# One-hots of a degree count in pairs of edge tiles, in a graph network kernel

## The chip, the cores and the metric

The kernel runs on one core of one Trainium2 chip. The metric is the device time of one execution in microseconds (us). A core has five engines with queues of their own: TensorE (PE, with its weight loads listed as PEld), VectorE (DVE), ScalarE (ACT), GpSimd (POOL) and SyncE (SP, which issues DMAs). They meet only at semaphores. SBUF, the on-chip memory, has 128 partitions.

## The reference

A graph of 12,500 nodes and 200,000 edges, sorted by destination, goes through two residual blocks: three layers of graph convolution, and one layer with edge features.

```python
loop = jnp.arange(N, dtype=message_edge.dtype)
src = jnp.concatenate([message_edge[0], loop])
dst = jnp.concatenate([message_edge[1], loop])
deg = jax.ops.segment_sum(jnp.ones_like(dst, dtype=jnp.float32), dst, num_segments=N)
dinv = jnp.where(deg > 0, jax.lax.rsqrt(deg), 0.0)
norm = dinv[src] * dinv[dst]
x = jax.nn.relu(_gcn_conv(node_embed, W1, b1, src, dst, norm))
# ... two more layers; then the layer with edge features:
msg = hv[src] * filt
h = jax.ops.segment_sum(msg, dst, num_segments=N_NODES)
return jax.nn.silu(h @ W_post.T + b_post)
```

The part that matters here is `deg`: how many edges end in each node.

## The kernel before, in words

Edges are laid out in tiles of 128, one edge per partition; 8 tiles (`BLOCK_TILES`) make a block, and there are 196 blocks (`BLOCKS`). A node number is split into a window (number / 128, 98 of them, `WINDOWS`) and a remainder (number mod 128).

After the loads and some integer arithmetic on VectorE (L846 to L875), the first long stage counts degrees. For every block VectorE writes two one-hot arrays in bf16 (loop at L878, through the helper `tile_hots`, whose instructions all stand at L695): `rem_hot`, 128 remainders for each of 8 tiles (1,024 elements a partition), and `win_hot`, 98 windows for each of 8 tiles (784 elements). Each compares a constant, `iota_block`, with the numbers of the block's edges (`dst_rem`, `dst_win`, one number per partition and tile). TensorE then multiplies, tile by tile, the remainders' one-hot (the weights, 128x128) with the windows' one-hot (the moving operand, 98 columns) and sums all 1,568 tiles in one PSUM area, `ps_deg` (`deg_block`, L1347 to L1352): the count of edges for each remainder and window.

In both arrays the tile index is the innermost one: element (n, k) of tile k stands at 8n + k. Tile k's operand is thus read at a step of 8 elements, 16 bytes.

The array `hot` has room for two blocks (index `a`). VectorE waits with `deg_used` until TensorE is done with the block two before; TensorE waits with `deg_hot` until VectorE has written the block. The constant `iota_block` (value n at every (n, k)) is written by GpSimd at L488 before anything else; it lies in the memory of `onehot_more`, by which name the profile lists it.

Behind the loop, in VectorE's program, come a short chain (L889 to L923), the copy of the counts, a layer norm and the first projection; then the dense stage with sub-window tables, whose helper is `tile_hots` again, with one or two tiles at a time (`src_extra`, `src_main`, on `stage_fn`, compared with `src_rem` from a first tile that is read from a table). Their order on TensorE, in a loop over 25 pairs of windows, does not depend on the degree count's layout. L1376 multiplies those arrays, L1389 the fp8 counts made from them; L1233 transposes node features before the projections at L1247.

Of the kernel before, what the change touches and what calls it, by code (L numbers as in the profile page):

```python
# [23 lines left out]
BF16 = mybir.dt.bfloat16  # L24
# [3 lines left out]
ALU = mybir.AluOpType  # L28
# [4 lines left out]
P = 128  # L33
NODES, EDGES, D, RADIAL = 12500, 200000, 64, 50
WINDOWS = -(-NODES // P)
# [5 lines left out]
BLOCK_TILES = 8  # L41
# [37 lines left out]
def gnn_program(nc, x, src, dst, radial, W1, b1, W2, b2, W3, b3, W_pre, b_pre, W_rad, b_rad, W_post, b_post, out):  # L79
    ctx = ExitStack()  # L80
    with ctx:
# [3 lines left out]
        def sem(name):  # L85
            return ctx.enter_context(nc.semaphore(name))

        def cut(buffer, at, n):

            return buffer[:, at:at + n]  # L90
# [30 lines left out]
        dst_rem = cut(ring, 2 * TILES, TILES // 2).bitcast(BF16)  # L121
        dst_win = cut(ring, 3 * TILES, TILES // 2).bitcast(BF16)
# [5 lines left out]
        hot = sbuf("hot", [P, 2 * BLOCK_TILES * SPAN])  # L128
        onehot = hot[:, :].rearrange("p (a k n) -> p a k n", a=2, n=SPAN)
        onehot16 = cut(hot, 0, BLOCK_TILES * SPAN).bitcast(BF16).rearrange("p (a k n) -> p a k n", a=2, n=SPAN)  # L130
        rest = cut(hot, BLOCK_TILES * SPAN, BLOCK_TILES * D).rearrange("p (k f) -> p k f", f=D)
        rem_hot = cut(hot, 0, BLOCK_TILES * P).bitcast(BF16).rearrange("p (a n k) -> p a n k", a=2, n=P)
        win_hot = cut(hot, BLOCK_TILES * P, BLOCK_TILES * WINDOWS).bitcast(BF16).rearrange(
            "p (a n k) -> p a n k", a=2, n=WINDOWS)
        stage_nf = cut(hot, 0, 2 * GROUP * D).rearrange("p (h w f) -> p h w f", h=2, f=D)
        gated = stage_nf
        onehot_more = sbuf("onehot_more", [P, BLOCK_TILES, MORE])
        more_flat = onehot_more[:, :, :].rearrange("p k n -> p (k n)")
        iota_block = cut(more_flat, 0, P * BLOCK_TILES // 2).bitcast(BF16).rearrange("p (n k) -> p n k", n=P)
        rel_more = sbuf("rel_more", [P, BLOCK_TILES])  # L140


# [45 lines left out]
        base = sbuf("base", [1, BLOCKS], I32)  # L188
# [33 lines left out]
        ps_deg = ps[:, 0, 0:WINDOWS]  # L222
# [21 lines left out]
        deg_hot = sem("deg_hot")  # L244
# [231 lines left out]
        @block.gpsimd  # L476
        def _(pool):

            nc.gpsimd.memset(xs[:, WINDOWS - 1, :], 0.0).then_inc(xs_cleared, 1)
            nc.gpsimd.memset(ident[:, :], 0.0).then_inc(consts_made, 1)  # L480
            nc.gpsimd.memset(one[:, :], 1.0).then_inc(consts_made, 1)
            nc.gpsimd.memset(found[:, :], 0.0).then_inc(consts_made, 1)
            nc.gpsimd.memset(sub_table[:, 2 * SUBS:], 0).then_inc(consts_made, 1)
            nc.gpsimd.iota(iota_i[:, 0:SPAN], pattern=[[1, SPAN]], base=0, channel_multiplier=0).then_inc(consts_made, 1)
            nc.gpsimd.iota(iota_i[:, SPAN:SPAN + WINDOWS], pattern=[[MORE, WINDOWS]], base=SPAN,
                           channel_multiplier=0).then_inc(consts_made, 1)

            nc.gpsimd.iota(iota_block, pattern=[[1, P], [0, BLOCK_TILES]], base=0, channel_multiplier=0,  # L488
                           allow_small_or_imprecise_dtypes=True).then_inc(consts_made, 1)
            nc.gpsimd.iota(sub_start[:, :], pattern=[[STRIDE, SUBS]], base=0, channel_multiplier=0,  # L490
                           allow_small_or_imprecise_dtypes=True).then_inc(consts_made, 1)
            nc.gpsimd.iota(block_no, pattern=[[1, BLOCKS]], base=0, channel_multiplier=0,
                           allow_small_or_imprecise_dtypes=True).then_inc(consts_made, 1)
            pool.wait_ge(consts_made, N_CONSTS - 1)
            nc.gpsimd.affine_select(out=ident[:, :], in_=ident[:, :], compare_op=ALU.not_equal, fill=1.0,
                                    base=0, pattern=[[-1, P]], channel_multiplier=1).then_inc(consts_made, 1)

            pool.wait_ge(block_range, 2)
            nc.gpsimd.partition_all_reduce(range_p1, range_p, P, REDUCE.max).then_inc(range_all, 1)

            pool.wait_ge(z_used, (PROJECT(0) + 1) * GROUPS + 2)
            nc.gpsimd.iota(iota_joint, pattern=[[1, JOINT]], base=0, channel_multiplier=0,
                           allow_small_or_imprecise_dtypes=True).then_inc(turns_made, 1)
            nc.gpsimd.iota(iota_main, pattern=[[1, P], [0, MAIN]], base=0, channel_multiplier=0,
                           allow_small_or_imprecise_dtypes=True).then_inc(turns_made, 1)

            def gather(at, i, j):
                pool.sem_inc(gather_turn, 1)
                for k in range(BLOCK_TILES):
                    c = j * BLOCK_TILES + k  # L510
                    nc.gpsimd.indirect_dma_start(  # L511
                        out=rows[:, j, k * D:(k + 1) * D], out_offset=None, in_=table[:, :],
                        in_offset=bass.IndirectOffsetOnAxis(ap=row_stage[:, c:c + 1], axis=0),
                    ).then_inc(gathered[j], 16)

            pool.wait_ge(table_written, 16 * GROUPS)
            pool.wait_ge(tail_known, 1)
            at = Pass(pool, FUSED)
            with pool.Fori(0, at.rounds) as i:
                for j in range(SLOTS):  # L520
                    pool.wait_ge(rows_staged, at.turn(i, j + 1))
                    pool.wait_ge(slot_free, at.turn(i, j + 1))
                    gather(at, i, j)

            pool.wait_ge(check_ready, 2)
            nc.gpsimd.partition_all_reduce(check[:, :], check_p[:, :], P, REDUCE.add).then_inc(check_all, 1)

            pool.wait_ge(mode_ready, 1)
            for p in range(PASSES):
                at = Pass(pool, p)  # L530
                if p:
                    pool.wait_ge(fn_staged, (COLLECT(p - 1) + 1) * GROUPS)
                    nc.gpsimd.memset(sumT[:, :], 0.0).then_inc(sums_cleared, 1)
                pool.wait_ge(table_written, 16 * GROUPS * (p + 1))
                with pool.If(at.rounds > 0) if p == REDO else nullcontext():
                    with pool.Fori(0, at.rounds) as i:
                        for j in range(SLOTS):
                            pool.wait_ge(rows_staged, at.turn(i, j + 1))
                            gather(at, i, j)
                if p == GCN_LAYERS - 1:  # L540

                    pool.wait_ge(sums_done, GCN_LAYERS)
                    nc.gpsimd.memset(radial_sb[:, :, :], 1.0).then_inc(radial_ones, 1)
# [105 lines left out]
        def _(dve):  # L649
# [43 lines left out]
            def tile_hots(to, columns, of):  # L693

                return nc.vector.tensor_tensor(to, columns, of.unsqueeze(1).to_broadcast(to.shape), ALU.is_equal)  # L695

            def split_rows(at, i, j):

                whole = rows[:, j, :].rearrange("p (k f) -> p k f", f=D)
                high, middle = split_upper[j % 2][:, :, 0:D], split_upper[j % 2][:, :, D:]  # L700

                def after(k):
                    dve.wait_ge(split_step, at.turn(i, j) * 3 + k)

                dve.wait_ge(gathered[j], at.gathers(i))
                nc.vector.tensor_copy(high, whole).then_inc(split_step, 1)
                dve.wait_ge(split_ready, at.turn(i, j + 1))
                after(1)
                nc.vector.tensor_tensor(rest, whole, high, ALU.subtract).then_inc(split_step, 1)
                after(2)  # L710
                nc.vector.tensor_copy(middle, rest).then_inc(split_step, 1)
                after(3)
                nc.vector.tensor_tensor(split_low[j % 2], rest, middle, ALU.subtract).then_inc(split_ready, 1)
# [164 lines left out]
            with dve.Fori(0, BLOCKS // 2) as b2:  # L878
                for a in range(2):

                    dve.wait_ge(deg_used, b2 * 2 + (a + 1))
                    tiles = bass.ds(b2 * (2 * BLOCK_TILES) + a * BLOCK_TILES, BLOCK_TILES)
                    tile_hots(rem_hot[:, a, :, :], iota_block, dst_rem[:, tiles])
                    tile_hots(win_hot[:, a, :, :], iota_block[:, 0:WINDOWS, :], dst_win[:, tiles]).then_inc(deg_hot, 1)

# [335 lines left out]
        def _(pe):  # L1223
# [123 lines left out]
            def deg_block(b, a, first, last):  # L1347
                pe.wait_ge(deg_hot, b + 1)
                for k in range(BLOCK_TILES):
                    d = nc.tensor.matmul(ps_deg, rem_hot[:, a, :, k], win_hot[:, a, :, k],  # L1350
                                         start=(first and k == 0), stop=(last and k == BLOCK_TILES - 1))
                d.then_inc(deg_used, 1)  # L1352

# [163 lines left out]
```

## Time and profile before

| | |
|---|---|
| median of 3 runs | 5896.86 us (5894.55 to 5936.55) |
| the profiled execution | 5911.64 us, span of its trace 5909.8 us |
| PE busy | 4498.9 us (76%) |
| DVE busy | 2831.0 us (48%) |
| POOL busy | 2942.4 us (50%) |
| ACT busy | 946.4 us (16%) |
| the degree count's stage | 48.8 to about 347 us |

Busy shares are means over stages with different limits. A matmul's end is modelled and matmuls are pipelined, so the step from one start to the next says more than the length of one. A line like "x8" in the timeline is a run of like instructions: its start, and the time from there to the end of the last.

### The profile page before, as it was taken

What the parts mean: (1) busy time and instruction counts of PE and PEld (TensorE: products, weight loads), DVE (VectorE), ACT (ScalarE), POOL (GpSimd) and SP (SyncE); (2) the same over time, 40 slices, a digit from 0 to 9 for tenths busy, and PEclk for the clock granted to TensorE, in tenths of its full rate; (3) what the DMA queues carried; (4) which work ended last, traced back from release to release, by engine and by line L of the source; (5) the groups of instructions that cost most, each with busy time, mean ns of one, the idle gap of its engine ahead of it and who ended that gap; (6) DMA issues with size and microseconds to landing.
All of it is one profiled execution on the core that took longest, in us unless ns stands there. A gap on an engine that the chain in (4) does not pass through costs nothing.

```text
span 5909.8 us, 111101 instructions
## 1 busy us (share of the span) xinstructions
PE 4498.9 (76%) x31388; PEld 3593.4 (61%) x31389; DVE 2831.0 (48%) x8076; ACT 946.4 (16%) x2182; POOL 2942.4 (50%) x3031
## 2 busy tenths in 40 slices
PE   6957777888888888999689996666666666666665
PEld 4743344555555558999689995655555555555554
DVE  6778777777777765222252222532222222222225
ACT  0001233344445552000010000100000000000002
POOL 0002233455510002777637775077777777777772
PEclk9998999999999996999869997566666666666665
DMA  1000011122211112555225553022222222222221
GB/s 34 0 9 20 30 44 57 59 63 71 73 61 67 67 67 73 178 178 177 66 87 178 179 177 78 22 46 47 46 47 47 47 46 47 47 46 47 47 47 32
DMA packets 158668, 407.12 MB, mean 69 GB/s; under 512 B 67564, under 2 KB 80940, under 8 KB 139124
## 3 DMA queue, kind: packets, MB, share of 16 engines
q1 hardware_dynamic: 62068, 305.32, 14.7%
q0 software_dynamic: 96256, 98.76, 8.7%
q14 instruction: 317, 2.60, 0.1%
q8 instruction: 27, 0.44, 0.0%
HBM read 307.53 MB, written 96.33 MB: 68 GB/s over the span
## 4 chain that ended last, share of the span: by engine, by line
PE 40%; POOL 26%; issue 18%; DVE 10%; DVEq 4%; DMA 1%; SPq 0%; ACT 0%; POOLq 0%; ACTq 0%
POOL rows_flat L511 26%; PE ps L1275 14%; PE ps L1255 6%; PE ps L1376 5%; PE ps L1350 5%; PE ps L1389 5%; PE ps L1247 4%; DVE sumT L980 4%; DVE stage_fn L695 1%; PE ps L1233 1%; DVEq L1055 1%; DVEq L695 1%; DVE hot L1213 1%; DVEq L980 1%; DVE hot L689 0%
## 5 line engine op out<-in xcount | busy, mean ns | idle before, releaser
L511 POOL DMA_INDIRECT rows_flat<-table,row_stage x3008 | 2897.1, 963 | 1710.8 <-issue 1600.0
L1255 PE MATMUL ps<-hot,msg_flat 128*64 128x160 f32 x3136 | 811.5, 446 | 717.1 <-DVE msg_flat L801 717.1
L1255 PEld LDWEIGHTS ps<-hot,msg_flat 128*64 128x64 f32 x3136 | 652.5, 216 | 832.3 <-issue 731.7
L1376 PE MATMUL ps<-sumT,stage_fn 128*128 128x392 f16 x3976 | 858.9, 336 | 333.3 <-DVE sumT L980 193.2
L980 DVE TENSOR_SCALAR sumT<-stage_fn,sub_start,sumT 128x784 f16<-128x784 f16 x1988 | 893.9, 484 | 4.6 <-issue 3.5
L1376 PEld LDWEIGHTS ps<-sumT,stage_fn 128*128 128x128 f16 x3976 | 311.6, 98 | 859.7 <-issue 561.2
L1275 PE MATMUL ps<-wide,ring 128*128 128x192 bf16 x9800 | 826.4, 246 | 0.0
L591 ACT ACTIVATE ring<-ps 128x784 fp8e4<-128x784 f32 x800 | 657.2, 822 | 1002.6 <-PE ps L1376 968.2
L1275 PEld LDWEIGHTS ps<-wide,ring 128*128 128x128 fp8e4 x9800 | 803.8, 98 | 22.7 <-issue 22.7
L689 DVE TENSOR_SCALAR hot<-iota,dst_rel 128x160 f32<-128x160 f32 x3008 | 702.4, 305 | 227.1 <-issue 183.5
L801 DVE TENSOR_TENSOR msg_flat<-rows_flat,ps 128x512 f32<-128x512 f32 x196 | 134.7, 687 | 1009.0 <-DMA rows_flat<-table,row_stage 1003.9
L695 DVE TENSOR_TENSOR stage_fn<-stage_fn,src_rem 128x256 f16<-128x256 f16 (+1 forms) x1188 | 398.0, 335 | 381.6 <-issue 213.5
L582 ACT COPY row_stage<-row_i 128x8 int32 x376 | 73.3, 196 | 3064.1 <-DVE sumT L721 3058.9
L1255 PE MATMUL ps<-hot,rows_flat 128*64 128x160 f32 x2880 | 464.7, 318 | 120.3 <-DMA rows_flat<-table,row_stage 67.8
L1255 PEld LDWEIGHTS ps<-hot,rows_flat 128*64 128x64 f32 x2880 | 401.4, 145 | 161.7 <-issue 141.8
L1319 PEld LDWEIGHTS ps<-w_rad,ring 51*128 51x128 f32 x3136 | 438.5, 220 | 58.8 <-issue 58.8
L1319 PE MATMUL ps<-w_rad,ring 51*128 51x64 f32 x3136 | 467.6, 309 | 0.0
L1389 PE MATMUL ps<-wide,ring 128*128 128x192 bf16 x4900 | 420.4, 246 | 2.2 <-issue 1.8
L1389 PEld LDWEIGHTS ps<-wide,ring 128*128 128x128 fp8e4 x4900 | 404.5, 98 | 22.7 <-issue 15.6
L721 DVE TENSOR_TENSOR sumT<-sumT,ps 64x160 f32 x376 | 117.9, 314 | 518.9 <-PE ps L1255 332.2
L748 DVE TENSOR_REDUCE dense_sum<-ps 128x64 f32<-128x192 f32 x150 | 53.4, 356 | 604.3 <-PE ps L1275 601.3
L1350 PE MATMUL ps<-hot 128*128 128x98 bf16 x1568 | 296.7, 360 | 50.1 <-DVE hot L695 50.1
(146 smaller groups left out, 2060.8 us busy)
## 6 DMA issues: line engine op xcount, KB each, us to landing
ring<-counts SPq DMA_DIRECT2D x100, 1568.0 KB
counts<-ring SPq DMA_DIRECT2D x50, 1568.0 KB, 6.3
rows_flat<-table,row_stage POOLq DMA_INDIRECT x3008
ring<-in_radial SPq DMA_DIRECT2D x196, 200.0 KB
table<-node SPq DMA_DIRECT2D x56, 224.0 KB, 1.9
out<-node SPq DMA_DIRECT2D x13, 224.0 KB
ring<-in_dst SPq DMA_DIRECT2D x1, 784.0 KB
ring<-in_src SPq DMA_DIRECT2D x1, 784.0 KB
```

Of the source, the lines that this page charges most:

```text
L511: nc.gpsimd.indirect_dma_start(out=rows[:, j, k * D:(k + 1) * D], out_offset=None, in_=table[:, :], in_offset=bass.IndirectOffsetOnAxis(ap ...
L591: nc.scalar.activation(to, of, ACT.Identity, scale=float(UNIT), saturate=True, accum_out=found_ring[:, h, t:t + 1]).then_inc(sub_copied, 1)
L689: one = nc.vector.tensor_scalar(to[:, k, :], columns, rel[:, bass.ds(tile0 + k, 1)], None, ALU.is_equal)
L695: return nc.vector.tensor_tensor(to, columns, of.unsqueeze(1).to_broadcast(to.shape), ALU.is_equal)
L980: return nc.vector.tensor_scalar(to, iota_joint, sub_start[:, bass.ds(sub, 1)], joint_of[:, bass.ds(t, 1)], ALU.add, ALU.is_equal)
L1247: z = nc.tensor.matmul(ps_z[:, h, i * D:(i + 1) * D], stage_fn[0:n, h, i * P:(i + 1) * P], w, start=True, stop=True)
L1255: s = nc.tensor.matmul(to, of, mats[:, k, :], start=(k == 0), stop=(k == BLOCK_TILES - 1))
L1275: d = nc.tensor.matmul(ps_dense[:, h, :], count_ring[:, h, q, :], parts[:, q, :], start=(q == 0), stop=(q == WINDOWS - 1))
L1319: f = nc.tensor.matmul(ps_filt[:, j % 2, k * D:(k + 1) * D], radial_sb[:, j, k * P:(k + 1) * P], w_rad[:, :], start=True, stop=True)
L1350: d = nc.tensor.matmul(ps_deg, rem_hot[:, a, :, k], win_hot[:, a, :, k], start=(first and k == 0), stop=(last and k == BLOCK_TILES - 1))
L1376: m = nc.tensor.matmul(to[:, c, :], sources[:, :, k], joint[k][:, c * (JOINT // 2):(c + 1) * (JOINT // 2)], start=first, stop=True, skip_g ...
L1389: d = nc.tensor.matmul(ps_dense[:, h, :], count_ring[:, h, q, :], parts[:, q, :], start=(q == 0), stop=(q == WINDOWS - 1))
```

## The change

The tile index is split in two: pair m (4 of them) and place k in the pair (2). The arrays become (m, n, k): in a pair, the two tiles' elements alternate, and one tile's operand is read at a step of 2 elements, 4 bytes. The constant has only two places per value and is repeated over the four pairs by the access pattern. The comparisons go through a new helper, `pair_hots`; the matmuls take the same tiles in the same order. The element counts of the comparisons, the number of instructions on each engine, their order and their waits stay. `tile_hots` stays for the later stage.

```diff
-        rem_hot = cut(hot, 0, BLOCK_TILES * P).bitcast(BF16).rearrange("p (a n k) -> p a n k", a=2, n=P)
+        rem_hot = cut(hot, 0, BLOCK_TILES * P).bitcast(BF16).rearrange("p (a m n k) -> p a m n k", a=2, n=P, k=2)
         win_hot = cut(hot, BLOCK_TILES * P, BLOCK_TILES * WINDOWS).bitcast(BF16).rearrange(
-            "p (a n k) -> p a n k", a=2, n=WINDOWS)
+            "p (a m n k) -> p a m n k", a=2, n=WINDOWS, k=2)
...
-        iota_block = cut(more_flat, 0, P * BLOCK_TILES // 2).bitcast(BF16).rearrange("p (n k) -> p n k", n=P)
+        iota_block = cut(more_flat, 0, P).bitcast(BF16).rearrange("p (n k) -> p n k", n=P)
...
-            nc.gpsimd.iota(iota_block, pattern=[[1, P], [0, BLOCK_TILES]], base=0, channel_multiplier=0,
+            nc.gpsimd.iota(iota_block, pattern=[[1, P], [0, 2]], base=0, channel_multiplier=0,
...
+            def pair_hots(to, columns, of):
+
+                return nc.vector.tensor_tensor(to, columns.unsqueeze(1).to_broadcast(to.shape),
+                                               of.rearrange("p (m k) -> p m k", k=2).unsqueeze(2).to_broadcast(to.shape),
+                                               ALU.is_equal)
...
-                    tile_hots(rem_hot[:, a, :, :], iota_block, dst_rem[:, tiles])
-                    tile_hots(win_hot[:, a, :, :], iota_block[:, 0:WINDOWS, :], dst_win[:, tiles]).then_inc(deg_hot, 1)
+                    pair_hots(rem_hot[:, a, :, :, :], iota_block, dst_rem[:, tiles])
+                    pair_hots(win_hot[:, a, :, :, :], iota_block[:, 0:WINDOWS, :], dst_win[:, tiles]).then_inc(deg_hot, 1)
...
-                    d = nc.tensor.matmul(ps_deg, rem_hot[:, a, :, k], win_hot[:, a, :, k],
+                    d = nc.tensor.matmul(ps_deg, rem_hot[:, a, k // 2, :, k % 2], win_hot[:, a, k // 2, :, k % 2],
                                          start=(first and k == 0), stop=(last and k == BLOCK_TILES - 1))
```

## Rows read from the trace of the kernel before

**Rows 1.** Chain of waits, 0 to 420 us: start us, us, what
```profile
50.08 293.66 PE ps L1350 x1552
```

**Rows 2.** Busy time by stretch: stretch, us, then busy us (instructions) by engine
```profile
core 0: us, PE busy (x) PEld busy (x) DVE busy (x) ACT busy (x) POOL busy (x), PEclk, DMA share, GB/s
48.80:347.00 298.20, 296.66 (x1568) 210.61 (x1568) 230.95 (x398) 0.00 (x0) 0.00 (x0) 1.00 0.00 0
```

**Rows 3.** Groups by shape, 48 to 347 us: count | busy us, mean ns | idle before
```profile
L1350 PE MATMUL ps<-hot 128*128 128x98 bf16 x1568 | 296.7, 360 | 50.1 <-DVE hot L695 50.1
L1350 PEld LDWEIGHTS ps<-hot 128*128 128x128 bf16 x1568 | 210.6, 147 | 135.4 <-issue 49.7 <-DVE hot L695 49.1
L695 DVE TENSOR_TENSOR hot<-onehot_more,ring 128x1024 bf16<-128x1024 bf16 x196 | 135.7, 693 | 67.2 <-PE ps L1350 67.2
L695 DVE TENSOR_TENSOR hot<-onehot_more,ring 128x784 bf16<-128x784 bf16 x196 | 109.7, 560 | 0.0
```

**Rows 4.** Waits, 48 to 347 us: us in total, times, longest
```profile
DVE hot L695 <- PE ps L1350: 67.2, 194, 0.8
PEld ps L1350 <- DVE hot L695: 49.1, 194, 0.3
```

**Rows 5.** Timeline, degree count: start us, us, instruction [idle before]
```profile
48.77 2.23 DVE L695 TENSOR_TENSOR hot<-onehot_more,ring 128x1024 bf16<-128x1024 bf16 x4
...
200.21 1.17 DVE L695 TENSOR_TENSOR hot<-onehot_more,ring 128x1024 bf16<-128x1024 bf16 x2 [0.43 <-PE ps L1350]
...
201.43 1.64 PE L1350 MATMUL ps<-hot 128*128 128x98 bf16 x8
...
203.24 1.17 DVE L695 TENSOR_TENSOR hot<-onehot_more,ring 128x1024 bf16<-128x1024 bf16 x2 [0.43 <-PE ps L1350]
```

**Rows 6.** Transposes by groups: 416-421, 421-434, 436-470 us; stretch 435-486 us
```profile
L1233 PE MATMUL ps<-ident,hot 128*64 128x128 f32 x14 | 3.2, 419 | 63.5 <-ACT hot L556 63.5
...
L1233 PE MATMUL ps<-ident,hot 128*64 128x128 f32 x35 | 4.8, 276 | 0.0
...
L1233 PE MATMUL ps<-ident,hot 128*64 128x128 f32 x49 | 11.9, 418 | 0.0
...
435.00:486.00 51.00, 42.12 (x180) 34.34 (x180) 36.59 (x66) 9.33 (x17) 7.44 (x7) 0.50 0.14 52
```

**Rows 7.** Timeline at 350 and 484 us, and groups of 478 to 486 us
```profile
350.93 2.83 PE L1365 MATMUL ps<-deg,pick 128*1 128x50 f32 x32 [4.19 <-DVE deg L927]
...
484.56 1.49 PE L1376 MATMUL ps<-sumT,stage_fn 128*128 128x392 f16 x4 [0.34 <-DVE sumT L980]
...
L1376 PE MATMUL ps<-sumT,stage_fn 128*128 128x392 f16 x10 | 3.6, 524 | 8.9 <-DVE sumT L980 8.9
L1376 PEld LDWEIGHTS ps<-sumT,stage_fn 128*128 128x128 f16 x10 | 0.9, 116 | 11.1 <-issue 8.7 <-DVE sumT L980 2.4
```

**Rows 8.** Groups of 487-569 and 2199-2211 us; timeline at 2199 us
```profile
L1376 PEld LDWEIGHTS ps<-sumT,stage_fn 128*128 128x128 f16 x224 | 13.2, 97 | 69.3 <-DVE sumT L980 62.0 <-issue 6.7
...
L1389 PEld LDWEIGHTS ps<-wide,ring 128*128 128x128 fp8e4 x142 | 11.7, 98 | 0.0
...
2198.85 12.29 PE L1389 MATMUL ps<-wide,ring 128*128 128x192 bf16 x147
```

**Rows 9.** Timeline, VectorE, at 600 us
```profile
599.60 0.42 DVE L695 TENSOR_TENSOR stage_fn<-stage_fn,src_rem 128x256 f16<-128x256 f16 x1
599.94 0.87 DVE L980 TENSOR_SCALAR sumT<-stage_fn,sub_start,sumT 128x784 f16<-128x784 f16 x2
...
603.69 0.29 DVE L695 TENSOR_TENSOR stage_fn<-stage_fn,src_rem 128x256 f16<-128x256 f16 x1 [0.19 <-issue]
603.90 0.87 DVE L980 TENSOR_SCALAR sumT<-stage_fn,sub_start,sumT 128x784 f16<-128x784 f16 x2
```

**Rows 10.** Groups, 0 to 48 us
```profile
L488 POOL IOTA onehot_more<- 128x1024 bf16 x1 | 1.9, 1927 | 0.0
L846 DVE CAST dst_rel<-ring 128x1568 f32<-128x1568 int32 x1 | 1.0, 977 | 29.0 <-DMA w_rad<-in_b_rad 29.0
```

## The prediction

> **What bounds the kernel now.** I read the chain of waits first. In the first 420 us one piece stands out: 293.7 us in which the chain runs through the degree count's matmuls at L1350 [rows 1]. I then asked for that stretch alone. TensorE is busy in all but 2 us of it, VectorE for 231 of 298 us, ScalarE, GpSimd and the DMA queues not at all [rows 2]. So the time of the stage is decided between two engines, and since VectorE's program runs on in order behind it, what the stage gives back the whole kernel gets back.
>
> The groups by shape give 196 blocks: two VectorE comparisons a block (693 and 560 ns), eight pairs of a weight load and a 98-column matmul (147 and 360 ns) [rows 3]. The waits are of both signs: VectorE waits for TensorE 194 times (67 us in total) and TensorE's loads wait for VectorE 194 times (49 us) [rows 4]. Neither engine alone sets the pace then. The timeline shows what does [rows 5]. The one-hots have two buffers, so block b+2 can only be written when block b has been multiplied. Follow one buffer round: VectorE starts at 200.21 and is done at 201.38 (1.17 us); TensorE starts at 201.43 (0.05 later) and takes 1.64; VectorE starts into the same buffer at 203.24 (0.17 after 203.07). That is 3.03 us for two blocks, 1.515 us a block; 196 of them make 297 us, which is the stage. TensorE's 1.64 us are seven steps of 0.183 and one whole matmul of 0.36: (1.64 - 0.36) / 7 = 0.183 us from one matmul to the next.
>
> The clock view prints 1.00 for the stage [rows 2], but I do not read it as a level. The transposes at L1233 take 419 ns at 416 to 421 us, as long as the 418 ns in a stretch granted 0.50 (1.2 GHz), and 276 ns right after [rows 6]. The 14 transposes at 416 to 421 us are (3.2 - 0.42) / 13 = 0.214 us apart for 128 float32 columns [rows 6], so 50 such columns make 0.084 at that level and half of it at the upper one; the 32 matmuls of 50 float32 columns at 350.9 us, 4 us after the stage, take 2.83 us, 0.088 each [rows 7]. I take the stage to run at the lower level.
>
> **The change part by part.** The edit moves no instruction: same counts, same shapes, same waits. Three things differ.
>
> *The constant of L488.* It is written with 256 elements for 1,024, 1.9 us of GpSimd. VectorE's first instruction waits until 29.0 us for a DMA of weights, behind which GpSimd's few constants are hidden [rows 10]. Price nothing; without the cover it would be a gain of about 1.4 us.
>
> *VectorE's two comparisons.* They write as many elements, in runs of two instead of eight. The nearest rows are the 128x256 comparisons at L695, which the kernel already lays out in pairs of edge tiles. They come at two speeds: one at 603.69 us is followed after 0.21 us by the next instruction, one at 599.60 after 0.34 [rows 9]. The step of 0.13 us is 256 elements at half the rate. I worked out the first tile of each of the 800 from the edges' destinations in the reference: it is even in 391 and odd in 409, and all the fast ones are even, all the slow ones odd. An odd first tile makes each pair straddle a 4-byte word. In the changed code a block starts at a multiple of eight tiles, always even. The fast row fits the present rate too: from 784 to 1,024 elements the duration grows by 133 ns, 0.55 ns an element [rows 3], and 256 of them are 0.14 us of the 0.21. So the price is between nothing and 1,808 x 0.13 / 256 = 0.92 us a block, and I take nothing. The Trainium skill speaks against my reading: its page "Vector Engine (DVE) Microarchitecture Reference", section 5.1, says that 4-byte alignment makes no difference to the packed mode with two sources. By that rule the slow half has another cause, and the new layout could catch it; the trace does not bear the rule out, since the speed goes with the parity in all but the few dozen that waited for something else.
>
> *TensorE's operands.* Weights and moving columns are now read at a step of 4 bytes instead of 16. On the weight side the trace has the price: L1376 loads 128 columns of 2 bytes, partly at a step of 4 bytes, in a mean of 116 ns at the lower clock [rows 7] against 147 ns here at 16; at the upper clock it needs 97 ns, as the fp8 loads without a step (98) [rows 8]. On the moving side no row shows a step of 4 bytes. Bounds: without any penalty 98 columns cost 0.081 us, by the 392-column matmuls at the lower clock, (1.49 - 0.52) / 3 = 0.323 us [rows 7], 0.82 ns a column; with all of today's penalty 0.183. I take 0.081, since the loads show that a step of 4 bytes costs the reading of weights nothing. A weight load of 128 columns fits beside a shorter matmul than it lasts: at 2,199 us 147 pairs take 12.29 us, 0.083 each, with loads of 98 ns [rows 8].
>
> The sum: TensorE's block becomes 8 x 0.081 + 0.20 = 0.85 us, where 0.20 is what a contiguous matmul lasts beyond its columns (0.524 - 0.323). The round of a buffer is 1.17 + 0.05 + 0.85 + 0.17 = 2.24, so 1.12 us a block. VectorE by itself needs 1.06 (two blocks without a wait take 2.23, a block 1.17, [rows 5]), so the round still decides, narrowly. Between the first start and the last lie 195 steps: 195 x (1.515 - 1.12) = 77 us. The profiled execution took 5911.6 us, so it would take 5835. It lies 14.8 us above the median of the three runs, 5896.86; from that the forecast is 5820 us, 1.3% less. Each 0.01 us of pace more costs 8 x 0.01 / 2 x 195 = 7.8 us. About 1% (59 us) is what a measurement of this kernel tells from no change; that is a pace of 0.104.
>
> **The rivals.**
>
> *Weight loads set the pace.* If a load has to end before the next pair can go on, the pace is what a load is seen to last at the lower clock, 0.112 to 0.116 [rows 7]: block 1.10 to 1.13, round 1.25, gain 51 to 53 us, 5845. For it: here loads are 147 ns and begin 0.18 apart, with few columns to hide them. Against it: the 0.083 pace of [rows 8] with loads of 98. The skill's page "TensorE: Matmul & The Clock Gate", section on LDWEIGHTS, gives columns / 1.2 ns, 107 ns for 128; by that the pace would be 0.107, the gain 57 us and the time 5840, but the row of 0.083 is shorter than that rule allows.
>
> *Only the weights profit.* The moving columns keep 0.183: gain 0, 5897. For it: the pace of 0.183 is longer than a load (0.147), so it is the columns that hold today. Against it: the loads at 4 bytes, read from the same memory. Partial cases lie between.
>
> *VectorE becomes the bound from its own side.* If TensorE's block falls under 0.73 us, as when its clock rises, the 1.06 us remain: gain 195 x 0.455 = 89 us, 5808. Against it: between 435 and 486 us TensorE was busy for 42 of 51 us and stayed at 0.50 [rows 6], and after the change it streams less densely.
>
> *Slower: the comparisons lose the packed rate.* With 0.92 us more a block VectorE needs 1.06 + 0.92 = 1.98, above the round: 195 x 0.465 = 91 us lost, 5988. It decides from 0.45 us more a block, 0.25 ns an element. For it: half of the rows in pairs are that slow. Against it: parity, and that GpSimd is idle here.
>
> **How the numbers follow.** My forecast 0.62, the loads' pace 0.15, weights alone 0.07, VectorE's bound 0.08, slower 0.08. Faster by over 1% takes the first and the fourth, 0.70; within 1% the second and third, 0.22; slower 0.08. The range must hold 0.8: from 5803 (VectorE's bound less 5 us of scatter) to 5860 (the loads' pace, and partial penalties up to a pace of 0.13). It leaves out weights alone and slower, 0.15. The forecast's own range is 5811 to 5830.
>
> **What the next profile shows.** Right: loads at L1350's successor about 105 to 120 ns, matmuls about 0.29 us and 0.08 apart, VectorE's two comparisons still 693 and 560 ns, its wait for TensorE down to about 12 us in total (195 x 0.06), TensorE idle for a quarter of the stage, the stage 220 us long. Wrong: comparisons of 1.2 and 0.95 us (the packed rate lost), matmuls still 0.18 apart (columns not helped), or 0.11 apart right behind each load (loads hold).

## The result and the profile after

The changed kernel takes 0.9866 of the time before (95% interval 0.9837 to 0.9896; medians 5851.0 and 5916.7 us, four runs each), so it is faster by 1.0 to 1.6%. Timed again later beside another kernel (e10 below), it took 0.9870 (0.9844 to 0.9895). The forecast was 5820 us against 5896.9, a ratio of 0.987. The four runs of the kernel before range from 5894.6 to 5937.6 us, so the ratio says more than the two medians.

The groups of the degree count after the change, where those of [rows 3] stood (count | busy us, mean ns | idle before). The new helper's comparisons stand at L699, the matmuls at L1356:

```profile
L1356 PE MATMUL ps<-hot 128*128 128x98 bf16 x1568 | 163.6, 279 | 103.7 <-DVE hot L699 103.7
L699 DVE TENSOR_TENSOR hot<-onehot_more,ring 128x1024 bf16<-128x1024 bf16 x196 | 134.9, 688 | 0.0
L1356 PEld LDWEIGHTS ps<-hot 128*128 128x128 bf16 x1568 | 121.8, 135 | 144.9 <-DVE hot L699 95.7 <-issue 49.3
L699 DVE TENSOR_TENSOR hot<-onehot_more,ring 128x784 bf16<-128x784 bf16 x196 | 109.5, 559 | 0.0
```

VectorE's comparisons last what they lasted (688 and 559 ns for 693 and 560). TensorE's matmuls went from 296.7 to 163.6 us of busy time. The waits, where those of [rows 4] stood (us in total, times, longest): VectorE's row of 67.2 us is gone, and TensorE now waits in every block. Of its 103.7 us, 49.6 are the wait for the first block, ahead of the stage; 54 us fall into the stage.

```profile
PE ps L1356 <- DVE hot L699: 103.7, 196, 49.6
PEld ps L1356 <- DVE hot L699: 95.7, 195, 0.6
```

Busy time of the stretch, as in [rows 2], from the first comparison to the last matmul:

```profile
48.30:267.30 219.00, 163.62 (x1568) 121.79 (x1568) 218.89 (x397) 0.00 (x0) 0.00 (x0) 1.00 0.00 0
```

The stage takes 219.0 us for 298.0, so it gives 79.0 us. The two profiled executions differ by 64.5 us (5909.8 to 5845.3). The missing 14.5 us lie behind the stage, 11 of them between the last float16 matmul and the last of the 192-column ones (1386.7 us before, 1397.9 after). That stretch took 1385.1 us in e3, 1386.7 in e6, 1397.5 in e4 and 1408.6 in e10 below, all with the same code there, so it varies by itself. In that stretch the transposes and the projections (L1233 and L1247 of the kernel before) come a second time. The rows of that work, before and after, as in [rows 2]:

```profile
2260.40:2316.80 56.40, 55.84 (x295) 48.58 (x295) 41.08 (x67) 19.07 (x30) 6.05 (x1) 0.62 0.14 53
2183.60:2250.60 67.00, 67.00 (x295) 57.62 (x295) 41.59 (x67) 19.06 (x30) 6.04 (x1) 0.50 0.12 45
```

The same work took 56.4 us at a mean granted clock of 0.62 before and 67.0 us at 0.50 after, which is 10.6 of the 11 us. e6 had 56.3 us at 0.62, e4 67.0 at 0.50. Why the clock rose there in some runs and not in others is not shown.

### The profile page after: what moved, and what is told of

It reads as the page before. It is cut to its first block, busy times and chain, and to the rows that moved or that the text cites. A ratio compares the mean times of both kernels' runs of the same rounds, so it can differ in the third digit from the quotient of the medians.

```text
span 5845.3 us, 111101 instructions
## 1 busy us (share of the span) xinstructions
PE 4378.9 (75%) x31388; PEld 3515.8 (60%) x31389; DVE 2819.8 (48%) x8076; ACT 946.0 (16%) x2182; POOL 2940.3 (50%) x3031
## 4 chain that ended last, share of the span: by engine, by line
PE 36%; POOL 26%; issue 20%; DVE 11%; DVEq 5%; DMA 1%; SPq 0%; ACT 0%; POOLq 0%; ACTq 0%
POOL rows_flat L511 26%; PE ps L1281 14%; PE ps L1261 6%; PE ps L1382 5%; PE ps L1395 5%; PE ps L1253 5%; DVE sumT L986 4%; DVE hot L699 2%; DVE stage_fn L695 1%; PE ps L1239 1%; DVEq L1061 1%; DVEq L695 1%; DVE hot L1219 1%; DVEq L986 1%; DVE hot L689 0%
## 5 line engine op out<-in xcount | busy, mean ns | idle before, releaser
L695 DVE TENSOR_TENSOR stage_fn<-stage_fn,src_rem 128x256 f16<-128x256 f16 (+1 forms) x1188 | 394.8, 332 | 382.5 <-issue 218.8
```

## The experiments

In all of them "stage" is the time from the first comparison's start to the last matmul's end, and "pace" the median step from one matmul's start to the next, both taken from the traces. e1 to e7 were run once each, and the total of one kernel differs by tens of us from run to run, so the stages are compared and not the totals; the changed kernel's stage took 219.0 us, and 218.8 when it was run again (e10).

### Which operand holds TensorE: e1 and e2

e1 lays out only the moving columns in pairs, e2 only the weights. Each needs both constants; the core of e1:

```diff
-                    pair_hots(rem_hot[:, a, :, :, :], iota_block, dst_rem[:, tiles])
-                    pair_hots(win_hot[:, a, :, :, :], iota_block[:, 0:WINDOWS, :], dst_win[:, tiles]).then_inc(deg_hot, 1)
+                    tile_hots(rem_hot[:, a, :, :], iota_block, dst_rem[:, tiles])
+                    pair_hots(win_hot[:, a, :, :, :], iota_pair[:, 0:WINDOWS, :], dst_win[:, tiles]).then_inc(deg_hot, 1)
...
-                    d = nc.tensor.matmul(ps_deg, rem_hot[:, a, k // 2, :, k % 2], win_hot[:, a, k // 2, :, k % 2],
+                    d = nc.tensor.matmul(ps_deg, rem_hot[:, a, :, k], win_hot[:, a, k // 2, :, k % 2],
```

and of e2:

```diff
-                    d = nc.tensor.matmul(ps_deg, rem_hot[:, a, k // 2, :, k % 2], win_hot[:, a, k // 2, :, k % 2],
+                    d = nc.tensor.matmul(ps_deg, rem_hot[:, a, k // 2, :, k % 2], win_hot[:, a, :, k],
```

e1, columns only. 

> Only the moving columns (windows) are laid out in pairs; the weights (remainders) stay in eights, read at a step of 16 bytes. Theory: the columns' reading sets TensorE's pace. Then loads stay at about 145 ns, the pace from matmul to matmul is 0.081 us as in the changed kernel, VectorE decides, and the stage from the first comparison to the last matmul takes 219 us (298 before, 219 changed). Rival: the loads set the pace. Then it is about 0.145, TensorE's block 1.36 us, the round 1.38 us a block, the stage 270 us.

e2, weights only. 

> Only the weights (remainders) are laid out in pairs; the moving columns stay in eights. Theory that the columns set the pace: pace 0.18 us, loads 105 to 145 ns, stage 297 us, nothing gained. Rival that the loads set it: pace near 0.11 to 0.15, stage 245 to 270 us.

The groups of e1:

```profile
L1359 PE MATMUL ps<-hot 128*128 128x98 bf16 x1568 | 171.5, 284 | 100.0 <-DVE hot L702 99.8
...
L1359 PEld LDWEIGHTS ps<-hot 128*128 128x128 bf16 x1568 | 133.0, 159 | 138.0 <-DVE hot L702 88.6 <-issue 49.3
```

and of e2:

```profile
L1359 PE MATMUL ps<-hot 128*128 128x98 bf16 x1568 | 289.5, 354 | 49.4 <-DVE hot L698 49.4
L1359 PEld LDWEIGHTS ps<-hot 128*128 128x128 bf16 x1568 | 173.3, 122 | 164.8 <-DVE hot L698 58.7 <-issue 49.0
```

e1 keeps slow loads (159 ns) and still runs at a pace of 0.082 us, TensorE's block 171.5 / 196 = 0.875 us, 1.133 us from block to block, stage 223.1. e2 has fast loads (122 ns) and stays at 0.176, 1.477 us a block, stage 290.8. The columns held TensorE; the weights' layout is worth 4 to 7 us of the stage, which the two expectations (219 and 297 us) had left out. The loads' pace as a rival falls too: in e1 a load lasts twice as long as the pace. Slow loads show only at the start of a block: e1's first step from matmul to matmul is 0.106 us for 0.066 in the changed kernel, which is the 0.04 us that its block is longer.

### How far the step may go: e3 and e6

e3 interleaves four tiles (a step of 8 bytes), e6 none (2 bytes); the edit is the group size:

```diff
-        rem_hot = cut(hot, 0, BLOCK_TILES * P).bitcast(BF16).rearrange("p (a m n k) -> p a m n k", a=2, n=P, k=2)
+        rem_hot = cut(hot, 0, BLOCK_TILES * P).bitcast(BF16).rearrange("p (a m n k) -> p a m n k", a=2, n=P, k=4)
```

with the same for `win_hot`, the constant, the helper and the matmuls' indices.

e3, fours. 

> Both arrays in fours, a step of 8 bytes. If reading is free as long as a 16-byte line gives two elements: pace 0.081 us, loads as in the changed kernel (105 to 142 ns), stage 219 us. If the price grows with the step in proportion: pace about 0.081 + 0.102 x 4/12 = 0.115 us, TensorE's block 1.12, the round 1.26 us a block, stage 246 us. VectorE's comparisons 0.69 and 0.56 us either way.

e6, singles. 

> No interleaving: every tile's one-hot contiguous (a step of 2 bytes), the numbers compared in runs of one. TensorE's pace 0.081 us, loads 105 to 142 ns as in the changed kernel. If a run of one costs VectorE the packed rate, as the 128x128 comparisons at L695 suggest (0.20 us to the next instruction, as long as 256 elements in aligned pairs): 1.22 and 0.97 us, stage 397 us. If it is kept: 219 us.

The groups of e3:

```profile
L1356 PE MATMUL ps<-hot 128*128 128x98 bf16 x1568 | 176.3, 272 | 97.2 <-DVE hot L699 97.1
L699 DVE TENSOR_TENSOR hot<-onehot_more,ring 128x1024 bf16<-128x1024 bf16 x196 | 135.0, 689 | 4.0
L1356 PEld LDWEIGHTS ps<-hot 128*128 128x128 bf16 x1568 | 131.5, 126 | 141.4 <-DVE hot L699 92.3 <-issue 49.2
```

and of e6:

```profile
L699 DVE TENSOR_TENSOR hot<-onehot_more,ring 128x1024 bf16<-128x1024 bf16 x196 | 237.7, 1213 | 0.0
L699 DVE TENSOR_TENSOR hot<-onehot_more,ring 128x784 bf16<-128x784 bf16 x196 | 188.8, 963 | 0.0
L1356 PE MATMUL ps<-hot 128*128 128x98 bf16 x1568 | 163.6, 281 | 282.0 <-DVE hot L699 282.0
```

With the kernels before and after, that makes a row by step: 2 bytes 0.081 us, 4 bytes 0.081, 8 bytes 0.092, 16 bytes 0.180 for 98 columns. Neither expectation of e3 holds: 8 bytes cost 0.011 us, a third of what growth in proportion would make, and not nothing. e3 moves both operands, but e1 kept its weights at 16 bytes and ran at 0.082, so the 0.011 us are put down to the columns. TensorE's block is 176.3 / 196 = 0.90 us, the step from block to block 1.145, the stage 225.3 us. Up to 4 bytes reading is free here, which is what the prediction took over from the weights' side.

e6 shows why the layout has pairs at all: with runs of one VectorE loses the packed rate (1,213 and 963 ns), its block takes 2.02 us and the stage 397.1, 99 us more than before.

### The price of an odd start: e4 and e5

Both move the edges' numbers by one element:

```diff
-        dst_rem = cut(ring, 2 * TILES, TILES // 2).bitcast(BF16)
-        dst_win = cut(ring, 3 * TILES, TILES // 2).bitcast(BF16)
+        dst_rem = cut(ring, 2 * TILES, TILES // 2 + 1).bitcast(BF16)[:, 1:TILES + 1]
+        dst_win = cut(ring, 3 * TILES, TILES // 2 + 1).bitcast(BF16)[:, 1:TILES + 1]
```

e4, on the changed kernel. 

> The changed kernel with the edges' numbers (dst_rem, dst_win) moved by one element of 2 bytes, so that every pair straddles a 4-byte word. If the two speeds at L695 come from that: comparisons of 1.22 and 0.97 us instead of 0.69 and 0.56, VectorE 2.05 us a block, stage 402 us, the kernel 183 us slower than the changed one. If alignment makes no difference to the packed mode: 0.69 and 0.56 us, stage 219 us.

e5, on the kernel before. 

> The kernel before, with the edges' numbers moved by one element of 2 bytes as in e4: runs of eight that start off a 4-byte word. If the packed rate hangs on the word alone: comparisons 1.22 and 0.97 us, VectorE 2.02 us a block, stage 397 us. If only runs of two suffer: 0.69 and 0.56 us, stage 298 us.

The groups of e4:

```profile
L699 DVE TENSOR_TENSOR hot<-onehot_more,ring 128x1024 bf16<-128x1024 bf16 x196 | 239.7, 1223 | 0.0
L699 DVE TENSOR_TENSOR hot<-onehot_more,ring 128x784 bf16<-128x784 bf16 x196 | 190.8, 973 | 0.0
```

and of e5:

```profile
L695 DVE TENSOR_TENSOR hot<-onehot_more,ring 128x1024 bf16<-128x1024 bf16 x196 | 161.7, 825 | 44.2 <-PE ps L1350 42.6
L695 DVE TENSOR_TENSOR hot<-onehot_more,ring 128x784 bf16<-128x784 bf16 x196 | 129.6, 661 | 0.0
```

e4 comes out as the parity said: 1,223 and 973 ns for 1.22 and 0.97 us, stage 397.1 for 402 us, total 6027 us for 5915 of the kernel before on the same chip. The rival that ended on the slower side was real, with its cause where [rows 9] had put it; the changed kernel escapes it because its blocks start at multiples of eight tiles.

e5 fits neither expectation, and tells more: runs of eight lose 132 ns in 1,024 elements and 101 in 784 (825 for 693, 661 for 560). There are 128 and 98 times 4 runs of two in a block's pairs, but 128 and 98 runs of eight. Per run that is 1.03 ns in both here, and (1223 - 688) / 512 = 1.04 and (973 - 559) / 392 = 1.06 in e4. So each run that starts off a 4-byte word costs about as much more as one pair of elements at the packed rate (2 x 0.55 = 1.1 ns, from [rows 3]); comparisons in pairs take 1.78 and 1.74 times as long, those in eights 1.2 times. The stage took 321.0 us. The round of a buffer gives (0.74 + 0.66 + 0.05 + 1.64 + 0.17) / 2 = 1.63 us a block, and 1.630 was measured.

### The clock and the round: e7

```diff
                 for k in range(BLOCK_TILES):
+                    nc.tensor.matmul(ps[:, 1, 0:WINDOWS], rem_hot[:, a, k // 2, :, k % 2], win_hot[:, a, k // 2, :, k % 2],
+                                         start=(first and k == 0), stop=(last and k == BLOCK_TILES - 1))
                     d = nc.tensor.matmul(ps_deg, rem_hot[:, a, k // 2, :, k % 2], win_hot[:, a, k // 2, :, k % 2],
```

> The changed kernel with every matmul of the degree count done twice, the second time into an unused PSUM area. If one buffer's round still decides: TensorE's block 16 x 0.081 + 0.20 = 1.50 us, the round (1.17 + 0.05 + 1.50 + 0.17) / 2 = 1.44 us a block, stage 283 us. If VectorE has decided alone since the change (its waits show as nothing), half of the added 0.65 us is hidden in TensorE's idle 0.26 us a block: pace-bound 1.30, stage 255 us. If the denser work raises TensorE's clock: pace 0.04 to 0.06, block 0.8 to 1.1, stage 219 to 245 us.

Its groups (the added matmuls stand at L1356, the others at L1358):

```profile
L1356 PE MATMUL ps<-hot 128*128 128x98 bf16 x1568 | 172.4, 211 | 95.6 <-DVE hot L699 95.5
L1358 PE MATMUL ps<-hot 128*128 128x98 bf16 x1568 | 169.8, 209 | 0.0
...
L699 DVE TENSOR_TENSOR hot<-onehot_more,ring 128x1024 bf16<-128x1024 bf16 x196 | 134.8, 688 | 6.8 <-PE ps L1358 1.1
```

and three matmuls of its timeline:

```profile
150.44 0.21 PE L1356 MATMUL ps<-hot 128*128 128x98 bf16 x1
150.48 0.21 PE L1358 MATMUL ps<-hot 128*128 128x98 bf16 x1
150.53 0.21 PE L1356 MATMUL ps<-hot 128*128 128x98 bf16 x1
```

Twice the matmuls, and the stage takes 228.1 us, 9 more than the changed kernel. A matmul lasts 210 ns instead of 279 and the pace is 0.047 us: the upper level, which the clock records give from 54.9 us on, 5 us after TensorE's first matmul. That is the third expectation (219 to 245 us). The three blocks that end ahead of 54.9 us still have a pace of 0.079 to 0.082: a stretch ahead of a trace's first clock record ran at the lower level here, although the view of stretches prints 1.00 for it. In the traces before and after, the first records come at 421.2 and 341.9 us, behind the stage. So the stage of the changed kernel does run at the lower level, as read from the neighbours in [rows 6, 7]. TensorE's block is 16 x 0.047 + 0.17 = 0.92 us and the round (1.17 + 0.05 + 0.92 + 0.17) / 2 = 1.155; 1.159 was measured.

### Fewer starts on VectorE: e9, beside e10

e10 is the changed kernel again. e9 gives each buffer 16 tiles:

```diff
+        deg_bufs = [cut(b, 0, WIDE * (P + WINDOWS) // 2) for b in (hot, rows_flat)]
+        rem_hot = [cut(b, 0, WIDE * P // 2).bitcast(BF16).rearrange("p (m n k) -> p m n k", n=P, k=2) for b in deg_bufs]
...
-            with dve.Fori(0, BLOCKS // 2) as b2:
+            with dve.Fori(0, BLOCKS // 4) as b4:
...
+                    tiles = bass.ds(b4 * (2 * WIDE) + a * WIDE, WIDE)
+                    pair_hots(rem_hot[a], iota_block, dst_rem[:, tiles])
+                    pair_hots(win_hot[a], iota_block[:, 0:WINDOWS, :], dst_win[:, tiles]).then_inc(deg_hot, 1)
```

e10. 

> The changed kernel itself, timed beside the next one. Stage 219 us, ratio to before about 0.987.

e9. 

> Pairs as in the changed kernel, but each buffer holds 16 tiles (the second buffer lies in the memory of rows_flat, which this stage leaves idle), so each comparison covers 2,048 or 1,568 elements and half as many are started and handed over. If what is left is VectorE's packed rate plus 0.07 us for each start: 1.14 + 0.89 = 2.02 us for 16 tiles; TensorE's block 16 x 0.081 + 0.20 = 1.50, the round (2.11 + 0.05 + 1.50 + 0.17) / 2 = 1.92, so VectorE alone decides; stage 98 x 2.02 + 2 = 200 us, 19 us less than the changed kernel, ratio to before about 0.983. If the handing over costs as much as before for each element, 219 us.

Groups of e9 (the second buffer has the same figures), its stretch of 48.3 to 248 us, and blocks of its timeline:

```profile
L701 DVE TENSOR_TENSOR hot<-onehot_more,ring 128x2048 bf16<-128x2048 bf16 x49 | 59.6, 1217 | 0.0
...
L701 DVE TENSOR_TENSOR hot<-onehot_more,ring 128x1568 bf16<-128x1568 bf16 x49 | 47.4, 968 | 0.0
```
```profile
48.30:248.00 199.70, 138.10 (x1568) 118.00 (x1568) 199.63 (x202) 0.00 (x0) 0.00 (x0) 0.60 0.00 0
```
```profile
60.55 1.49 PE L1358 MATMUL ps<-rows_flat 128*128 128x98 bf16 x16 [0.53 <-DVE rows_flat L701]
62.57 0.92 PE L1358 MATMUL ps<-hot 128*128 128x98 bf16 x16 [0.54 <-DVE hot L701]
64.59 0.92 PE L1358 MATMUL ps<-rows_flat 128*128 128x98 bf16 x16 [1.10 <-DVE rows_flat L701]
...
151.49 1.49 PE L1358 MATMUL ps<-hot 128*128 128x98 bf16 x16 [0.53 <-DVE hot L701]
153.51 1.49 PE L1358 MATMUL ps<-rows_flat 128*128 128x98 bf16 x16 [0.53 <-DVE rows_flat L701]
```

The stage is 199.7 us, the blocks 2.02 us apart, and TensorE's block 1.49 where the clock is low: each number as worked out. The ratio to before is 0.9833 (0.9809 to 0.9857), against 0.9870 (0.9844 to 0.9895) for e10 on the same chip; medians 5826.4 and 5845.2 us. The two intervals overlap a little, but the 18.8 us between the medians agree with the 19.2 between the stages, so this version is taken for the fastest of the three. Here the clock records reach into the stage. The first one, at 62.0 us, grants 1.00, and until 222.4 us five stretches of 1.00, 27 us in all, alternate with stretches of 0.50. A block takes 0.92 us in the former (matmuls 0.048 us apart) and 1.49 in the latter (0.081), and 1.49 ahead of 62.0 us too. The blocks stay 2.02 us apart either way: VectorE alone sets the pace, and a faster TensorE only waits longer (1.10 us for 0.53). The 0.60 that the view prints counts the first 14 us as 1.00, so it is too high.

## Why the prediction was right, point by point

**Who sets the pace.** The round of a buffer was the right thing to count. The timeline after, where [rows 5] stood (VectorE first, then TensorE):

```profile
150.17 0.56 DVE L699 TENSOR_TENSOR hot<-onehot_more,ring 128x784 bf16<-128x784 bf16 x1
150.70 0.69 DVE L699 TENSOR_TENSOR hot<-onehot_more,ring 128x1024 bf16<-128x1024 bf16 x1
151.31 0.56 DVE L699 TENSOR_TENSOR hot<-onehot_more,ring 128x784 bf16<-128x784 bf16 x1
151.78 0.68 DVE L699 TENSOR_TENSOR hot<-onehot_more,ring 128x1024 bf16<-128x1024 bf16 x1
152.39 0.56 DVE L699 TENSOR_TENSOR hot<-onehot_more,ring 128x784 bf16<-128x784 bf16 x1
152.92 0.69 DVE L699 TENSOR_TENSOR hot<-onehot_more,ring 128x1024 bf16<-128x1024 bf16 x1
```
```profile
150.78 0.84 PE L1356 MATMUL ps<-hot 128*128 128x98 bf16 x8 [0.25 <-DVE hot L699]
151.92 0.84 PE L1356 MATMUL ps<-hot 128*128 128x98 bf16 x8 [0.30 <-DVE hot L699]
```

TensorE ends a block at 151.62 and at 152.76; VectorE's next 1,024-element comparison starts 0.16 us later each time (151.78, 152.92). From the second comparison's start to the first one of the next block it takes 0.48 and 0.53 us in turn (medians 0.477 and 0.537). The 0.48 is what VectorE needs; the 0.05 to 0.06 more is a wait. Its rows show none, because an instruction's recorded end lies behind the start of the next one, so a wait shorter than that overlap (0.08 us) leaves no idle time. e1, e3 and e7 stretch the longer of the two steps to 0.58, 0.60 and 0.62 us as TensorE's block grows. e4 and e6, where VectorE alone decides, have 0.885 both times; the loop's own turn costs nothing.

**The sum.** TensorE's block was forecast at 0.85 us and is 0.84 (pace 0.081 as forecast, drain 0.279 - 0.081 = 0.20). The step from block to block was forecast at 1.12 and is 1.112. The stage gives 79.0 us for 77. The comparisons' price was nothing, and is nothing, with the row that could have spoken against it explained by e4. The lower level, which the sum took for TensorE, held for the whole stage; the records of e7 and e9 show that it need not have.

**What was off, without changing the sum.** I expected VectorE's wait down to about 12 us in total; the view shows none, and the steps above make about 98 x 0.06 = 6 us, hidden in the overlap. The 1.06 us that VectorE needs by itself were read too low: without a wait its comparisons start 0.605 and 0.477 us apart, 1.08 a block, so the round leads by half of what was thought and VectorE as the bound would have given 84 us and not 89. I expected loads of 105 to 120 ns and they average 135: the first of a block takes about 105, the second 117, those beside running matmuls about 142; the mean of 116 in [rows 7] mixes such kinds too (six loads of 102 to 105 ns, two of 118, two of 151). They do not hold the pace, so it did not matter. The 0.112 us in the price of the loads' pace stands in no row of [rows 7], which has 116 ns; with that alone the price is a gain of 50 us.

The median of 5851.0 us lies in the range, but above the 5811 to 5830 that was the forecast's own, and closer to the 5845 of the loads' pace than to 5820. The total can't tell these two apart: the fourth run of the kernel before moved its median from 5896.9 to 5916.7, and some 11 us behind the stage come and go with the clock. The pace and the length of the stage tell them apart. That the ratio agrees to three digits is in part luck; that the stage does is not.

**The rivals.** That loads set the pace: refuted by e1. The Trainium skill (page "TensorE: Matmul & The Clock Gate", section on LDWEIGHTS) gives a load columns / 1.2 ns, by estimate 107 ns for 128 columns. That does not bound the pace here, which is 0.081 us at the lower clock and 0.047 at the upper. That only the weights profit: refuted by e2, where they alone were changed and the stage gave 7 us. VectorE as the bound: not here, where the round still leads by 0.03 us a block, but in e9 it is. The blocks of e9 show it: their distance does not change with TensorE's clock. Slower by the packed rate: the mechanism is there (e4), and only the even start keeps it away. The Trainium skill (page "Vector Engine (DVE) Microarchitecture Reference", section 5.1) has alignment to 4 bytes make no difference to the packed mode. In this case's runs an odd start adds three quarters to the time of pairs (e4) and a fifth to that of eights (e5), so the measurement decides.

## What to carry to other kernels

A matmul's moving operand of two-byte elements could be read at a step of 4 bytes for nothing at the lower clock (0.081 us at 2 and at 4 bytes); at 16 it held TensorE to less than half its rate. Whether 4 bytes are free at the upper clock too, where they gave 0.047 us, no run shows, since none has these columns without a step there. The layout is chosen by whoever writes it, so look for the smallest group that still keeps the writer's packed rate. When two engines both show waits, follow one buffer round: the sum of both engines' times and the two handovers, divided by the number of buffers, is the pace, and it fits seven kernels here (before, after, e1, e2, e3, e5, e7) within 0.02 us a block. Before trusting a packed two-byte comparison, see whether its short runs start on a 4-byte word.

## What the runs showed of the hardware that was not expected

- A two-byte comparison pays about 1.04 ns more for each innermost run of its broadcast operand that starts off a 4-byte word: 688 to 1,223 ns with 512 runs of two, 693 to 825 ns with 128 runs of eight (e4, e5).
- A step of 8 bytes is not quite free for moving columns: 0.092 us for 98 columns, against 0.081 at 4 bytes and 0.180 at 16 (e3).
- TensorE stays at the lower clock for all of the changed kernel's stage, in which it is busy for 163.6 of 219 us, and rises 5 us after the first matmul when each is done twice; its pace goes from 0.081 to 0.047 us and the doubled work costs the stage 9 us (e7). In e9, busy for 138 of 200 us, it rises and falls five times.
- A granted clock of 1.00 in the view of stretches is no reading of the level ahead of a trace's first clock record: e9's blocks took 1.49 us until that record, at 62.0 us, and 0.92 behind it.
